# Adapter rows stacked by batch, and two small products on 64-row tiles of TensorE

## What is computed

```python
x = x + einsum('bct,bcd->bdt', x, L0_cond_weights[itok_B_1_198])
H     = einsum('btd,od->bto', x, W)
xa    = einsum('btd,brd->btr', x, A[itok_B_0_6])        # rank 16
delta = einsum('btr,bor->bto', xa, Bm[itok_B_0_6]) * scalings[itok_B_0_6]
x = x + H + delta
```

## Time and profile before

| | before |
|---|---|
| median of 3 runs | 821.88 us (821.73 to 821.96) |
| the profiled execution, its own time | 821.71 us |
| its span, first to last instruction | 819.8 us |
| PE, matmuls busy | 776.4 us (95% of the span), 5216 of them |
| PE, weight loads busy | 714.1 us (87%) |
| DVE busy | 537.9 us (66%) |
| ACT busy | 383.0 us (47%) |
| POOL busy | 152.8 us (19%) |

### The profile page before, as it was taken

How to read it: one execution, slowest core, us unless ns; L and a number is a source line. 1 busy time by engine, 2 the same in 40 slices (tenths; PEclk the granted TensorE clock), 3 DMA queues, 4 the chain that set the end, 5 groups by cost and what they waited for, 6 DMA issues and landing times.

```text
span 819.8 us, 16303 instructions
## 1 busy us (share of the span) xinstructions
PE 776.4 (95%) x5216; PEld 714.1 (87%) x5216; DVE 537.9 (66%) x921; ACT 383.0 (47%) x712; POOL 152.8 (19%) x297
## 2 busy tenths in 40 slices
PE   0489999999999999999999999999999999999996
PEld 0479999999999999999999999999999999999995
DVE  4965667666666766666677666666666667666663
ACT  3634454544444444444454544545444454544442
POOL 4620122221012222102222201222220122221000
PEclk9889999999999999999999999999999999999999
DMA  7043323333322333332233333233333223333211
GB/s 288 0 136 110 102 86 116 134 134 116 120 83 99 118 134 131 106 130 79 101 125 134 128 109 114 76 114 131 134 128 109 97 89 115 134 134 113 67 59 78
DMA packets 43748, 92.50 MB, mean 113 GB/s; under 512 B 7380, under 2 KB 23764, under 8 KB 43220
## 3 DMA queue, kind: packets, MB, share of 16 engines
q1 hardware_dynamic: 43588, 92.30, 32.5%
q10 hardware_dynamic: 144, 0.00, 0.0%
HBM read 58.72 MB, written 33.55 MB: 113 GB/s over the span
## 4 chain that ended last, share of the span: by engine, by line
PE 93%; DVE 3%; DMA 2%; SPq 1%; issue 0%; ACT 0%; DVEq 0%
PE beta L625 35%; PE delta L641 22%; PE beta L638 11%; PE alpha L625 11%; PE o_ps L669 4%; PE o_ps L667 4%; PE o_ps L668 4%; PE delta L649 2%; DMA w_raw<-wB 1%; DVE w_raw L567 1%; PE alpha L652 1%; PE beta L652 1%; DVE wn_lo L574 1%; DVE wr_lo L570 1%; PE xaT_ps L679 0%; DMA out<-o_sb 0%
## 5 line engine op out<-in xcount | busy, mean ns | idle before, releaser
L310 POOL TENSOR_TENSOR wr_lo<-a_ride,wr_hi 128x192 fp32r<-128x192 f32 x32 | 21.2, 664 | 608.2 <-ACT wr_hi L352 608.2
L625 PE MATMUL beta<-wr_hi,s_hi 128*128 128x256 f32 (+1 forms) x512 | 105.7, 288 | 13.1 <-DVE xa_part L484 12.4
L625 PE MATMUL beta<-wr_lo,s_hi 128*128 128x256 f32 (+1 forms) x512 | 105.1, 287 | 0.0
L625 PE MATMUL beta<-wr_hi,s_lo 128*128 128x256 f32 (+1 forms) x512 | 105.1, 286 | 0.0
L641 PE MATMUL delta<-wn_hi,s_hi 128*128 128x512 f32 x256 | 103.1, 403 | 0.0
L641 PE MATMUL delta<-wn_hi,s_lo 128*128 128x512 f32 x256 | 100.4, 392 | 0.0
L641 PE MATMUL delta<-wn_lo,s_hi 128*128 128x512 f32 x256 | 100.1, 391 | 0.0
L558 DVE COPY o_sb<-o_ps 128x512 f32<-128x512 f32 x64 | 43.8, 684 | 83.1 <-PE o_ps L669 80.3
L625 PEld LDWEIGHTS beta<-wr_hi,s_hi 128*128 128x128 f32 x512 | 83.3, 191 | 16.1 <-issue 12.6
L625 PEld LDWEIGHTS beta<-wr_lo,s_hi 128*128 128x128 f32 x512 | 81.4, 191 | 0.0
L625 PEld LDWEIGHTS beta<-wr_hi,s_lo 128*128 128x128 f32 x512 | 80.9, 190 | 0.0
(11 more groups left out here) (118 smaller groups left out, 1885.8 us busy)
## 6 DMA issues: line engine op xcount, KB each, us to landing
out<-o_sb SPq DMA_DIRECT2D x64, 512.0 KB, 2.7
x_even<-xT SPq DMA_DIRECT2D x32, 512.0 KB, 4.0
x_odd<-xT SPq DMA_DIRECT2D x32, 512.0 KB, 4.0
b_raw<-lora_b SPq DMA_DIRECT2D x192, 64.0 KB, 2.1
w_raw<-wB SPq DMA_DIRECT2D x4, 1024.0 KB, 8.8
a_now<-lora_a SPq DMA_DIRECT2D x64, 64.0 KB, 2.3
c_raw<-cond_w SPq DMA_DIRECT2D x64, 64.0 KB, 1.9
s_tab<-scalings ACTq DMA_DIRECT2D x1, 4.0 KB, 2.8
```

Source lines behind the costliest of these rows:

```text
L310: nc.gpsimd.tensor_tensor(ride_of(wr_lo, J1, J2), a_ride[:, :, 0:3, :], ride_of(wr_hi, J1, J2), ALU.subtract).then_inc(ride_ready, 1)
L625: last = nc.tensor.matmul(bank[:, h, 0:hi - lo], left[:, chunk + k, :], right[:, k, lo:hi], start=opens and k == 0 and left is left_hi and ...
```

## The change

The rows of `b_stack` are laid out by batch: rows 0 to 63 hold batch 0 (16 rows high, 16 rows high again, 16 rows low, 16 rows of zeros) and rows 64 to 127 batch 1 in the same way. The columns of `xa_cols` follow. `g_first` is gone: batch 0 alone is now rows 0 to 63 of `g_both` and `b_stack`, and batch 1 alone rows 64 to 127 of `g_second`. The product into `delta` and the two halves of the one into `alpha` are issued with these 64 rows, and both behind one wait for `g_both`. The low part of `b_stack` is now two DVE operations of 16 rows, and `b_ready` counts both.

```diff
@@ load_b, SP
-                    sp.wait_ge(b_ready, done(i, j, d - 1))
+                    sp.wait_ge(b_ready, done(i, j, d - 1, 2))
...
-                    for row in (32 * n, 32 * n + R, 64 + 32 * n):
+                    for row in (64 * n, 64 * n + R, 64 * n + 2 * R):
@@ step, ACT
-                    nc.scalar.activation(g_second[:, :], xaT_ps[:, 0:P], ACT.Copy, scale=mask[:, 1:2]).then_inc(g_ready, 1)
-                    nc.scalar.activation(g_first[:, :], xaT_ps[:, 0:P], ACT.Copy, scale=mask[:, 0:1]).then_inc(g_ready, 1)
-                    nc.scalar.activation(g_both[:, :], xaT_ps[:, 0:P], ACT.Copy, scale=mask[:, 2:3]).then_inc(g_ready, 1)
+                    nc.scalar.activation(g_second[:, :], xaT_ps[:, 0:P], ACT.Copy, scale=mask[:, 0:1]).then_inc(g_ready, 1)
+                    nc.scalar.activation(g_both[:, :], xaT_ps[:, 0:P], ACT.Copy, scale=mask[:, 1:2]).then_inc(g_ready, 1)
@@ step, DVE
-                    nc.vector.tensor_tensor(b_stack[64:112, :], b_raw[64:112, :], b_stack[64:112, :], ALU.subtract)\
-                        .then_inc(b_ready, 1)
-
-                    twice = xa_cols[:, :].rearrange("p (t s r) -> p s t r", t=2, r=R)
+                    for row in (2 * R, 64 + 2 * R):
+                        nc.vector.tensor_tensor(b_stack[row:row + R, :], b_raw[row:row + R, :], b_stack[row:row + R, :],
+                                                ALU.subtract).then_inc(b_ready, 1)
+
+                    twice = xa_cols[:, :].rearrange("p (n t s r) -> p n s t r", n=2, t=2, r=R)
@@ start, DVE: four memsets of mask in place of twelve
+            nc.vector.memset(mask[0:64, 0:1], 0.0).then_inc(mask_ready, 1)
+            nc.vector.memset(mask[0:64, 1:2], 1.0).then_inc(mask_ready, 1)
+            nc.vector.memset(mask[64:P, 0:1], 1.0).then_inc(mask_ready, 1)
+            nc.vector.memset(mask[64:P, 1:2], -1.0).then_inc(mask_ready, 1)
@@ step, PE
-                    pe.wait_ge(b_ready, done(i, j, 0))
-                    pe.wait_ge(g_ready, done(i, j, -1, 3) + 1)
-                    lora(delta, g_second, H).then_inc(d1_done, 1)
-                    pe.wait_ge(g_ready, done(i, j, -1, 3) + 2)
-                    lora(alpha, g_first, 0).then_inc(alpha_done, 1)
+                    pe.wait_ge(b_ready, done(i, j, 0, 2))
+                    pe.wait_ge(g_ready, done(i, j, 0, 2))
+
+                    second, head = slice(64, P), slice(0, 64)
+                    nc.tensor.matmul(delta[:, :], g_second[second, :], b_stack[second, H:T], start=False, stop=True,
+                                     skip_group_check=True).then_inc(d1_done, 1)
+                    for h in range(2):
+                        last = nc.tensor.matmul(alpha[:, h, 0:Q], g_both[head, :], b_stack[head, h * Q:(h + 1) * Q],
+                                                start=False, stop=True, skip_group_check=True)
+                    last.then_inc(alpha_done, 1)
...
-                    pe.wait_ge(g_ready, done(i, j, 0, 3))
                     lora(delta, g_both, H).then_inc(delta_done, 1)
```

More of the change, by code:

```diff
@@ L70, in cond_resid_kernel @@
         ident = sb("ident", [P, P], f32)
-        mask = sb("mask", [P, 3], f32)
+        mask = sb("mask", [P, 2], f32)
         xa_part = sb("xa_part", [P, R], f32)
@@ L74, in cond_resid_kernel @@
         xa_cols = sb("xa_cols", [P, P], f32)
-        g_first = sb("g_first", [P, P], f32r)
         g_second = sb("g_second", [P, P], f32r)
@@ L386, in step @@
                     if not exists(i, j, -1):
-                        act.wait_ge(mask_ready, 12)
-                    nc.scalar.activation(g_second[:, :], xaT_ps[:, 0:P], ACT.Copy, scale=mask[:, 1:2]).then_inc(g_ready, 1)
-                    nc.scalar.activation(g_first[:, :], xaT_ps[:, 0:P], ACT.Copy, scale=mask[:, 0:1]).then_inc(g_ready, 1)
-                    nc.scalar.activation(g_both[:, :], xaT_ps[:, 0:P], ACT.Copy, scale=mask[:, 2:3]).then_inc(g_ready, 1)
+                        act.wait_ge(mask_ready, 4)
+                    nc.scalar.activation(g_second[:, :], xaT_ps[:, 0:P], ACT.Copy, scale=mask[:, 0:1]).then_inc(g_ready, 1)
+                    nc.scalar.activation(g_both[:, :], xaT_ps[:, 0:P], ACT.Copy, scale=mask[:, 1:2]).then_inc(g_ready, 1)
                     act.wait_ge(d1_done, done(i, j, 0))
@@ L501, in step @@
                         dve.wait_ge(zeros_ready, 2)
-                    nc.vector.tensor_copy(twice[:, 0, :, :].bitcast(f32r),
+                    nc.vector.tensor_copy(twice[:, 0, 0, :, :].bitcast(f32r),
                                           xa_first[:, :].unsqueeze(1).to_broadcast([P, 2, R])).then_inc(xa_hi_ready, 1)
@@ L517, in step @@
                     dve.wait_ge(j6_done, done(i, j, 0))
-                    nc.vector.tensor_copy(twice[:, 2, :, :].bitcast(f32r),
+                    nc.vector.tensor_copy(twice[:, 1, 0, :, :].bitcast(f32r),
                                           xa_second.unsqueeze(1).to_broadcast([P, 2, R])).then_inc(xa_hi_ready, 1)
                     dve.wait_ge(xa_hi_ready, done(i, j, 0, 2))
-                    nc.vector.tensor_tensor(xa_cols[:, 3 * R:4 * R].bitcast(f32r), xa_second, xa_cols[:, 2 * R:3 * R],
+                    nc.vector.tensor_tensor(xa_cols[:, 64 + R:64 + 2 * R].bitcast(f32r), xa_second, xa_cols[:, 64:64 + R],
                                             ALU.subtract).then_inc(xa_ready, 1)
@@ L677, in transpose_xa @@
                     if not first:
-                        pe.wait_ge(g_ready, done(i, j, -1, 3))
+                        pe.wait_ge(g_ready, done(i, j, -1, 2))
                     nc.tensor.transpose(xaT_ps[:, 0:P], xa_cols[:, :], ident[:, :]).then_inc(xaT_done, 1)
```

## The result

| | before | after |
|---|---|---|
| median | 821.81 us (4 runs, 821.57 to 821.96) | 833.55 us (4 runs, 833.32 to 833.77) |
| ratio | | 1.0144, 95% interval 1.0129 to 1.0159 |
| profiled execution, span | 821.71, 819.8 us | 833.75, 831.9 us |
| one pair in the loop, transpose to transpose | 24.07 us | 24.38 us |

The account below looks back on a forecast made before the run. PE's row and the chain over ACT and DVE meet at J7, and the chain decides: 28 x (0.25 + 0.06) + 4 x 0.25 = 9.7 us, forecast 831.5 us, range 828.8 to 835.5, own mechanism 829.3 to 832.6.

Parts of the forecast that it names:

- What bounds it: In the loop, PE busy all the time and a path over other engines reach J7 together; lengthening either is paid in full.
- the chain over ACT and DVE to J7: Transpose over g, product into delta, ACT's copy, DVE's sum, then J7; claimed decisive, with slack 0.01 us at J7.
- the three waits: PE's loop waits for g_second, g_first and DVE's sum ahead of J7: slack 0.01, 0.03 us already lost, slack 0.01.
- The wait, + 0.25 a pair: Product into delta waits for ACT's second copy, ending at 223.65 in place of 223.40, in all 32 pairs.
- The form of the wait, + 0.06 in the loop: Two waits on the delta product's matmul in place of one, new in 28 loop steps; bounds 0 and 0.07 us.
- The products: LoRA products into delta and alpha on 64 rows: PE saves 0.06 to 0.29 us, a gap ahead of J7, worth 0.
- Leaving and entering: Changing to 64-row form and back around the LoRA products: 0 side by side; + 0.50 a pair if emptying, one after another.
- Rival A: Tiles at the LoRA products run one after the other and PE empties at the exit: 16 us, 837.8; chance 0.15 with smaller forms.
- B: Path from delta product to ACT's copy has give, kernel gets faster, 814.3; chance 0.03 in full, 0.04 partial.
- C: Tiles follow each other without emptying; still 831.5, gap ahead of J7 0.07 against 0.30; shares the forecast's chance of 0.76.
- DVE and SP at nothing: DVE's second low-part operation, 1.22 us, covered by 2.57 idle; SP's issues after b_ready 1.22 later; both cost 0.
- the signs named beforehand: In the profile after: pair 24.37 us, delta load idle 0.45 to 0.5, delta copy at 1.27, matmul idle before delta and J7.

## Why the prediction was right

*What bounds it.* The length of a pair was forecast at 24.37 us and is 24.38, and the wait was paid in full. That it is the chain over ACT and DVE to J7 that makes it so is only half right. The wait stands in front of a matmul of PE, and PE's own row carries 0.29 of the 0.31 up to the last matmul ahead of J7, where the two paths meet again within a few hundredths. No run has the joint wait without the chain. What the chain holds by itself is small where it was tried: taking J7's wait out of the kernel before brought 0.04 a pair. The slack was also read too finely. I had 0.01, 0.03 and 0.01 for the three waits; the two for g cost 0.03 together, J7's 0.04, and all three 0.09.

*The wait, + 0.25 a pair.* Right, and shown alone: 24.32 against 24.07.

*The form of the wait, + 0.06 in the loop.* Right, and shown alone: 0.067. It was read from the four steps outside the loop in the profile before. That it comes new in the loop alone holds too: the second and the last pair, which are written out, grew by 0.26 and 0.27 (from 24.12 to 24.38 and 24.39), those of the loop by 0.31.

*The products.* Their worth of 0 is right for this kernel: 24.38 with the tiles and 24.38 without. The reason given was another: PE's saving of 0.06 to 0.29 was to become a gap of 0.07 to 0.30 ahead of J7. There was no saving to hide, because the way out of the tiles took it: from the product into `delta` to the sixth matmul of `condition` PE took 1.69 us (227.53 to 229.22), and 1.67 before.

*Leaving and entering.* I had the entry at 0 because the wait covers it, and the exit, side by side, at J7 0.02 under the chain. That branch is what happened: J7's load starts at 229.40 behind L528 and its matmul at 229.46, and PE's own row comes there at 229.22 + 0.23 = 229.45. That it stays under the chain is luck in part: the margin is a hundredth or two, and a way out longer by 0.1 would have made each pair longer. Rival A's + 0.50, for tiles one after the other, was a little too high: 0.39 in that form without any cover. An entry does not wait for the end of the record of the matmul before it (0.39) but starts the load 0.32 after its start. The Trainium skill's rule (TensorEngine Tiling (Array Packing), section Key Properties), that a change of the tiling mode empties TensorE while tiles of one mode run independently, agrees in both halves with the runs with one tile, two in the same rows, and two side by side: 0.38 a pair for in and out, and 0.24 less when two run side by side. Whether TensorE is quite empty in between no profile shows, as the ends of its matmuls are modelled. Rival A, which needed the tiles one after the other, is out; B too, since the copy of `delta` came 1.27 after `g_second`, 1.28 without the tiles; C is out by the starts of the two products. C's sign, a small gap ahead of J7, would have misled: the gap is 0.01 with the tiles side by side.

*DVE and SP at nothing.* DVE's second operation is shown alone. For SP the list of PE's waits has no new row, and a pair came out as forecast without it; it was not tried alone.

*What was missing.* The sum was 9.7 us and the profiled execution 12.0 longer. The loop and the waits account for 9.8 of it. Beside them stand 1.5 us of low clock in the first pair, which no step of the prediction spoke of, 0.2 ahead of the first transpose and 0.7 behind the last copies; what the last two come from was not tried. The prediction gave 829.3 to 832.6 as the range of its own mechanism, and 833.55 lies above it; the wider range to 835.5 holds it, but that was widened for rival A and not for the clock. Without the low clock the two kernels with the same length of a pair measured 831.66 (idle time filled) and 832.16 us (tiles undone).

Of the signs named beforehand these were there: the pair of 24.38, the copy of `delta` 1.27 after `g_second`, the load idle 0.5, and `alpha` starting with `delta`. The idle time in front of the matmuls was not: 0.11 in a pair where 0.3 in front of the product was named, since the records of the matmuls overlap it, and none in front of J7. By the prediction's own words no idle time of J7's matmul and a longer pair would mean that PE's own row decides and A is right. The first half of this may be so, as said above; A is not.

## What to carry to other kernels

When PE is busy all the time and yet some of its weight loads idle a tenth or two of a microsecond, look for waits that end just when PE gets there. Here three of them cost 0.09 us a pair together, though no matmul showed as idle. A change that moves a wait one instruction earlier pays it in full in each round of the loop, so put the wait of a second product behind the first: here that is 24.23 against 24.31 us a pair. Two tiles side by side must save more than the way in and the way out cost: here two products gave 0.24 us against 0.38. And when a delay is put down to a chain over other engines, count PE's own row from start to start as well before you say which of the two it is.

## What the runs showed of the hardware

A change between products on 128 rows and on 64 rows of the array costs 0.38 us for in and out together, at full clock (24.36 us a pair with one tiled product, 23.98 with none). Two products on different halves of the rows start at the same time (both at 221.98 in the run with the chain taken out), two on the same half 0.34 us apart, and the pair is 0.24 longer. A matmul that waits for two semaphores, in place of one, starts its load 0.06 to 0.07 us later after the last of them (0.11 against 0.05).
